# Attention stage of a macaron block: score and value units regrouped, projections in two banks and three units ahead, one denominator pass per sequence

## The reference

```python
x = x + 0.5 * ffn(_layernorm(x))
x = x + attn(_layernorm(x))
x = x + 0.5 * ffn(_layernorm(x))
...
# attn: 16 heads of 64
Q = _phi(h @ Wq); K = _phi(h @ Wk); V = h @ Wv     # _phi(x) = elu(x) + 1, h = layernorm of the layer's input
num = causal sum of (q . k) v;  den = max(causal sum of (q . k), EPS_DEN)
x = x + (num / den) @ Wo
x = x + gelu(_layernorm(x) @ Wf1) @ Wf2
```

## Time and profile before

| what | us |
|---|---|
| median of 3 runs | 2244.29 |
| lowest, highest | 2234.66, 2257.18 |
| the profiled execution | 2249.25 |
| its span, first to last instruction | 2246.5 |
| mean granted TensorE clock, share of full speed | 0.926 |

### The profile page before, as it was taken

The page is one execution under the profiler, slowest core; times in us unless marked ns, Lnnn a source line. Parts: engine busy times, 40 slices in busy tenths (PEclk is TensorE's granted clock), DMA queues, the critical chain, the costliest instruction groups (busy, mean ns, idle before and its releaser), DMA issues. The chain is left out here.

```text
span 2246.5 us, 36234 instructions
## 1 busy us (share of the span) xinstructions
PE 1800.2 (80%) x12619; PEld 1410.7 (63%) x12619; DVE 1527.2 (68%) x4255; ACT 1027.5 (46%) x1754; POOL 949.2 (42%) x1035
## 2 busy tenths in 40 slices
PE   3341799993999999999999999999984342999970
PEld 2231677772777777777777777777763232777750
DVE  6663577774777777777777777777756563777753
ACT  1210566662455554554555545545531111766650
POOL 5775255556232323322323323232215774455560
PEclk9999999996999999999999999999995555999995
DMA  5533566651000000000000000000000114566637
GB/s 159 174 123 110 198 241 238 228 196 52 11 6 11 10 6 11 11 6 11 11 6 11 6 10 11 1 1 1 1 1 29 45 49 166 197 225 226 227 133 228
DMA packets 89310, 190.29 MB, mean 85 GB/s; under 512 B 15869, under 2 KB 54442, under 8 KB 78122
## 3 DMA queue, kind: packets, MB, share of 16 engines
q1 hardware_dynamic: 60202, 141.68, 18.8%
q0 software_dynamic: 18176, 37.79, 4.9%
q10 hardware_dynamic: 10752, 8.52, 1.1%
HBM read 131.08 MB, written 56.85 MB: 84 GB/s over the span
## 5 line engine op out<-in xcount | busy, mean ns | idle before, releaser
L503 POOL DMA_INDIRECT expert_rows<-f_rows_out,f_dest x312 | 311.3, 998 | 304.3 <-DVE f_rows_out L722 231.4
L1273 DVE TENSOR_TENSOR at_sc<-at_s_ps,at_mask 128x384 f32<-128x384 f32 x516 | 262.9, 551 | 139.4 <-PE at_s_ps L944 134.3
L1087 ACT ACTIVATE at_exps<-at_proj_ps 128x512 f32<-128x512 f32 x258 | 153.5, 595 | 369.0 <-PE at_proj_ps L925 362.3
L1165 POOL TENSOR_TENSOR at_sc<-at_sc 128x512 f32<-128x512 f32 x129 | 177.1, 1373 | 306.4 <-DVE at_sc L1273 303.9
L497 POOL DMA_INDIRECT sent_rows<-f_xn,f_slot x256 | 251.1, 981 | 107.7 <-issue 73.0
L435 ACT ACTIVATE f_hid<-f_up_ps,f_w 128x512 f32<-128x512 f32 x312 | 214.6, 688 | 171.5 <-PE f_up_ps L344 149.2
L1267 DVE SCALAR_TENSOR_TENSOR at_qk<-at_exps,at_relus 128x512 f32<-128x512 f32 x260 | 208.6, 802 | 53.2 <-ACT at_relus L1088 53.0
L699 DVE TENSOR_TENSOR f_hid_lo<-f_hid,f_hid_hi 128x512 fp32r<-128x512 f32 x312 | 208.2, 689 | 14.5
L941 PE MATMUL at_s_ps<-at_qk 64*128 64x256 f32 x1032 | 181.3, 428 | 3.4 <-DVE at_sc L1273 2.7
L955 PE MATMUL at_num_ps<-at_sc,at_vals 128*64 128x256 f32 x1024 | 160.5, 392 | 0.0
L695 DVE CAST f_hid_hi<-f_hid 128x512 fp32r<-128x512 f32 x156 | 66.6, 427 | 132.9 <-issue 121.6
(11 more groups left out here) (263 smaller groups left out, 4523.9 us busy)
## 6 DMA issues: line engine op xcount, KB each, us to landing
f_w<-split_weights SPq DMA_DIRECT2D x78, 1028.0 KB
f_got<-sent_rows SPq DMA_DIRECT2D x78, 264.0 KB
split_weights<-f_split SPq DMA_DIRECT2D x8, 1024.0 KB
at_taken<-expert_rows SPq DMA_DIRECT2D x64, 128.0 KB, 2.1
f_w<-expert_rows SPq DMA_DIRECT2D x32, 256.0 KB, 4.1
expert_rows<-f_rows_out,f_dest POOLq DMA_INDIRECT x312
sent_rows<-f_pads ACTq DMA_DIRECT2D x16, 264.0 KB
x<-in_L_attn_x SPq DMA_DIRECT2D x16, 256.0 KB, 5.6
```

The source lines that it names most:

```text
L503: g.indirect_dma_start(out=k.back[:, :], out_offset=bass.IndirectOffsetOnAxis(dest[:, i % RING_DEST, q:q + 1], 0), in_=rows_out[:, i % RIN ...
L1087: A(exps[:, c % 2, :], bank[:, :], ACT.Exp).then_inc(s_exp, 1)
L1165: g.tensor_tensor(sc[:, par, :, 3, :], sc[:, par, :, 1, :], sc[:, par, :, 2, :], ALU.add).then_inc(s_sum, 1)
L1273: last = tt(flat(sc[:, par, 2 * cc + half, 0:3, :]), s_ps[2 * cc + half][:, 0:3 * P], flat(mask[:, :, :]), ALU.mult)
```

## The change

- PE's order in a unit becomes S, S, V, then qk, qk, v. S and V, which use the array in parts, stand together; the three projections, which use all of it, stand together. Most fills move into or behind the projections.
- The projections use two banks in turn (proj_ps[0], proj_ps[1]; the second is the former den_ps) and run three units ahead. A projection waits until the one before the last has been evacuated.
- denominators runs once for a sequence, with 16 matmuls, at u = 0 of the next one between the two S. It writes the bank num_ps, so it waits for the copy of the last V, and the next V waits for DVE to have read it (s_den). at_sc grows from 2 to 6 buffers for this; at_num moves into the spent raw1 and raw2.
- The iterations run to NB + 2 with what each has to do (has_z, has_rest, has_down), so nothing runs on zeros and nothing for sequences past the last; there is no separate tail. The fills' order is up2, b0, down, b1, b2, b3, out, z and an (one transposing fill), up0. The four final broadcasts, which had a bank each, go through at_slot_ps one by one.
- hT_hi and h2_hi are made by ACT with a second affine instead of a cast on DVE.
- POOL's memsets of gel, xa, num and y go. It clears the first FFN's semaphores after s = 0, not at the end.

```diff
-        proj_ps, num_ps, den_ps, slot_ps = ps("proj"), ps("num"), ps("den"), ps("slot")
+        proj_ps, num_ps, slot_ps = [ps(f"proj{i}") for i in range(2)], ps("num"), ps("slot")
...
+            def project(what):
+                n = number[what]
+                bank = proj_bank(n)
+                if n >= 6:
+                    pe.wait_ge(s_proj_out, n - 5 if n < 8 else n - 1)
...
+            def denominators(s):
+                pe.wait_ge(s_sum, UNITS * (s + 1))
+                pe.wait_ge(s_num_out, UNITS * (s + 1))
+                for u in range(UNITS):
+                    for j in range(4):
+                        last = mm(num_ps[32 * j:32 * j + 32, 0:BT], den_sel[:, u, :], sc[:, (UNITS * s + u) % RING_SC, j, 0:4:3, :],
+                                  start=(u == 0), stop=(u == UNITS - 1))
+                last.then_inc(s_quad, 1)
...
+                    if u == 2 and has_rest(s):
+                        pe.wait_ge(s_o, 4 * (s - 1) + 4)
+                        output_product((s - 1) % 2)
+                    if ("qk", g + 3, 0) in number:
+                        project(("qk", g + 3, 0))
+                    if u == 1 and has_rest(s):
...
+                        broadcast(1)
+                    if ("qk", g + 3, 1) in number:
+                        project(("qk", g + 3, 1))
+                    if u == 1 and has_rest(s):
+                        pe.wait_ge(s_o, 4 * (s - 1) + 2)
+                        broadcast(2)
...
+                    if u == 0 and has_rest(s):
...
+                        broadcast(0)
+                    if u == 1 and has_rest(s):
+                        pe.wait_ge(s_o, 4 * (s - 1) + 3)
                         broadcast(3)
...
+                    if ("qk", g + 3, 0) in number:
+                        phi(2 * (g + 3))
...
+                    if u == 1 and rest:
+                        weigh(s, 1)
...
+                    if u == 1 and rest:
+                        weigh(s, 2)
+                        weigh(s, 3)
```

More of the change, by code:

```diff
@@ L767 @@
 RING_TAKEN = 4
+RING_SC = 6
 def attention_phase(nc, k, spent):
@@ L848, in attention_phase, with projected, proj_bank, has_z @@
             sem("gelu"), sem("x"))
-        fills_before = (0, 2, 5, 7)
-        first_banks = [proj_ps, s_ps[0], s_ps[1], s_ps[2]]
-        first_fills = [("qk", 0), ("qk", 1), ("v", 0), ("qk", 2), ("qk", 3), ("v", 1)]
+        LAST = UNITS * NB
+        first = [("qk", 0, 0), ("qk", 0, 1), ("v", 0, 0, 0), ("qk", 1, 0), ("qk", 1, 1), ("qk", 2, 0), ("qk", 2, 1), ("v", 0, 0, 1)]
+        def projected(g):
+            s, u = g // UNITS, g % UNITS
+            there = [("qk", g + 3, cc) for cc in range(2) if g + 3 < LAST]
+            ahead = s + (u + 2) // UNITS
+            return there + ([("v", ahead, ((u + 2) // 2) % 2, u % 2)] if ahead < NB else [])
+        number = {what: n for n, what in enumerate(first + [w for g in range(LAST) for w in projected(g)])}
+        def proj_bank(n):
+            return (proj_ps + s_ps)[n] if n < 6 else proj_ps[n % 2]
+        def has_z(s):
+            return s + 2 < NB
+        def has_rest(s):
+            return 1 <= s <= NB
+        def has_down(s):
+            return 2 <= s <= NB + 1
+        def fills(s):
+            return (["up2"] * has_down(s) + ["b0"] * has_rest(s) + ["down"] * has_down(s) + ["b1", "b2", "b3", "out"] * has_rest(s)
+                    + ["z_an"] * (has_z(s) or has_rest(s)) + ["up0"] * has_rest(s))
+        def fill(s, what):
+            return 3 + sum(len(fills(i)) for i in range(s)) + fills(s).index(what)
         def xc(s, q=None):
@@ L913, in output_product @@
                         cols = slice((c % 2) * BT + q * P, (c % 2) * BT + (q + 1) * P)
[L914 removed]
+                        last = mm(slot_ps[:, q * P:(q + 1) * P], num[par][:, c // 2, cols], k.wo[:, c, :],
                                   start=(c == 0), stop=(c == PAIRS - 1))
                 last.then_inc(s_slot, 1)
[L918 to L925, removed]
[L926 removed]
@@ L968, in denominators @@
                 last.then_inc(s_quad, 1)
-            pe.sem_inc(s_quad, 1)
             pe.wait_ge(s_z, 1)
[L972 to L986, removed]
+            transpose_slot()
@@ new lines, in affine, with z_out, gelu @@
+            def affine(dst, g_col, bank, s):
+                A(dst, bank, ACT.Identity, bias=k.cols[:, g_col + 1:g_col + 2], scale=k.cols[:, g_col:g_col + 1]).then_inc(s, 1)
+            def z_out(i):
+                if i >= 1:
+                    act.wait_ge(s_hT_lo, i)
+                affine(hT[:, :], ROW_G1, slot_ps[:, 0:BT], s_hT)
+                affine(hT_hi[:, i % 2, :], ROW_G1, slot_ps[:, 0:BT], s_hT_hi)
+            def gelu(s, what, c):
+                act.wait_ge(s_slot, fill(s, what))
+                A(flat(gel[:, c:c + 2, :]), slot_ps[:, :], ACT.Gelu).then_inc(s_gelu, 1)
@@ new lines, in _ @@
+                    if u == 3 and ahead:
+                        hT_low(s + 2)
+                    if u == 2 and rest:
+                        dve.wait_ge(s_st["C"], s)
+                        aggregate("C")
+                    if ("qk", g + 3, 0) in number:
+                        phi(2 * (g + 3))
+                    if u == 0 and ahead:
+                        dve.wait_ge(s_st["A"], s + 3)
+                        aggregate("A")
+                    if u == 0 and rest:
+                        weigh(s, 0)
```

505 lines of the change are left out of this document (221 added, 284 removed).

## The result

| | before | after |
|---|---|---|
| median us (range, runs) | 2250.73 (2234.66 to 2265.46, 4) | 2300.07 (2290.30 to 2306.97, 4) |
| span of the profiled execution | 2246.5 | 2305.0 |
| from attention's first transposition to its last sum | 1142.3 | 1184.5 |

The ratio is 1.022, 95% interval 1.013 to 1.031: slower, though the interval leaves open whether by more than 2%, and the median is 2 us beyond the upper end of the predicted range. Run again, the same two kernels gave 1.017 (1.012 to 1.022).

A forecast was written before the change was run, and what follows sets the result against it. PE was taken to bound the loop. +29.0 for 29 sequences, -9.9, -1.8 and -4.0 for first, second and last, -1.2 start and +6.4 end gave +18.5: 2267.8 on the profiled execution, 2263 on the median; range 2215 to 2298.

The forecast's parts named there:

- Changes of shape and D: PE, whole-array to part-array switches: 24 a sequence become 12 at 0.2 each, plus 0.1 for lost exits: -2.5 us.
- the four restarts: PE: a matmul run that starts after a wait is 0.1 longer; four a sequence, +0.4 us, lower bound none.
- Rival 4: PE: the 0.2 belongs to blocks, not shape changes, so the 2.4 stay: +3.4 a sequence, 2333 us; chance 0.02.
- Rival 2: Part-array shapes follow each other freely and waits cost no restart: +0.3 a sequence, 2243 us, no change; chance 0.20.
- v, +1.45: PE's v waits for the first qk's bank: 0.64 at u = 2 and 0.8 at u = 0, a sequence.
- Rival 1: Two projection banks hide the evacuation, v never waits: a sequence at 33.7, 2215 us, faster; chance 0.17.
- b2 and b3, +2.0: At u = 1 b2 waits 1.75 for weigh(1), queued behind phi on DVE; b3 waits 0.25 for weigh(2).
- Rival 3: POOL's work falls on DVE's chain through their shared port: +0.7 before b2, 2295 us, clearly slower; chance 0.18.
- A sequence, +1.0: The loop's period: the terms sum to +1.05, taken as +1.0, 35.35 us, for 29 sequences +29.0.
- The tail, +6.4: From the last V's end to the last sum: 32 us instead of 25.7, broadcasts going one by one; +3 to +9.
- Start, first and last sequence: Outside the steady loop: start -1.2 (-4 to +3), first sequence -9.9, second -1.8, last -4.0 us.

The follow-up runs named there:

- the run with two more: Changed kernel with u = 2's first qk between the two scores, output product behind V: 35.735 us a sequence, against 35.36 with the output product between the two qk.
- the filled wait: Changed kernel with the second qk's six matmuls at u = 1 issued three times, ahead of b2: steady intervals 35.41 to 35.47 us, attention 1172.7.
- the longer one: Changed kernel with DVE making the phi ahead of weigh(1) twice, so b2 waits longer: 37.28 to 37.55 us in every steady interval.
- the tail's banks: Changed kernel with the last pass's b1 to b3 in three scores banks, ahead of the down product: last V to last sum 28.9 us, 8.8 less.

## Why the prediction was wrong

The direction and the two waits were right; the size was not. Attention became 42.2 longer, by the steps it should have been 18.5. Point by point:

- **Changes of shape and D, -2.5.** Held in the main: 0.19 a change by the run with two more, so 2.3 for the 12, and D's successor starts after 1.86 (1013.63 to 1015.49), the number predicted. The count of 24 before missed two: at u = 3 half of the up product stands between V and D. Added up by the starts of all blocks of one sequence (before from 1009.06, after from 1049.83), what is no wait became 1.8 less, or 2.2 without the four restarts: 0.3 under the 2.5. Rival 4 falls by this. Rival 2 falls by the period, 1.1 over before's instead of 0.3; V takes 1.45 behind scores as it did behind a projection, so S to V is not free.
- **v, +1.45.** Held: 0.63 + 0.76 = 1.39 against 0.64 + 0.8. Rival 1, that two banks hide the evacuation, falls. The Trainium skill, Perfetto Trace Analysis, Optimizing Tensor Performance, asks that independent matmul groups rotate through different banks, so that the evacuation of one overlaps the next group. The changed kernel does so, and the trace agrees in part: the waits L969 <- L1114 of 0.47 and 0.60 show that two banks in this order hid only part of the evacuation. The prediction called the rule the opposite of its reading, which is more than it says. Putting v first removed both waits without a third bank.
- **b2 and b3, +2.0.** Held: 1.55 for b2 (1.75 said), and 0.25 for b3 (1030.66 to 1031.61 less 0.70), as said. Rival 3's port was not in this chain: phi and weigh there took 0.69 and 0.68. That 2300 lies near its 2295 is chance. Of its two witnesses the cast in rows 10 is the weaker: it ended at 547.89, 1.84 behind the memset named, while POOL's other memsets ran on to 547.74.
- **A sequence, +1.0.** 35.45 instead of 35.35, 29 x 0.1 = 3 us. That it is so near is in part luck: the waits came out 0.3 smaller and the gain 0.3 smaller than said. PE was busy for 93%, not below 92%.
- **The step that failed: the sum has no term for the clock.** I priced b2's wait at its length. PE's granted clock falls behind it in seven sequences, 7 x 1.6 = 11.3 us. Shown by the filled wait (work added, none slow) and the longer one (every one slow). The profile of before could have warned. In its tail, behind an idle of 3.01 (though not behind the one of 2.05 before it), PE ran at the lower level:

```profile
1667.55 3.81 PE L914 MATMUL at_slot_ps<-wo,at_num 128*128 128x128 f32 x32 [2.05 <-DVE at_num L1280]
1674.37 0.69 PE L882 MATMUL at_slot_ps<-ident,at_an 128*128 128x128 f32 x2 [3.01 <-DVE at_an L1248]
```

```profile
1675.00:1680.00 5.00, 2.99 (x13) 2.64 (x12) 0.72 (x2) 1.69 (x3) 0.00 (x0) 0.50 0.00 0
```

- **The tail, +6.4.** +12.0 (37.7 for 25.7). The order and the waits were as said; what I left out is in the main again the clock, and 4 of the 8.8 us that the tail's banks gave back are that. The bound of +9 was too near.
- **Start, first and last sequence.** PE's first projection came 3.8 sooner (544.63 for 548.43), as said, but the first scores of the loop start at 560.65 for 560.91, 0.3 sooner instead of 1.2: PE waits 5.6 there, for what was not found out, and starts again at half clock (its first part takes 1.22, 0.77 before). The first sequence took 26.3, not 24.4, but before's own had been 35.9 and not the 34.35 that I set against it, so it gave 9.6 of the 9.9; the second gave 1.65 of 1.8. The last, to its last V, took 30.2 instead of 28.8, and before's 31.3 instead of 32.8: -1.1 for -4.0. Together +4.2.

The terms are 3 + 11.3 + 5.6 + 4.2 = 24.1, where 42.2 - 18.5 = 23.7 are to be explained. Of these the clock is 11.3 in the loop and some 4 in the tail; without the loop's share alone the median would lie within the range. What the medians differ by beyond that (49.3 against 42.2) is within the scatter outside attention.

## What to carry to other kernels

A wait that is new on the bound engine costs its length and perhaps, as here behind idles of 1.4 and 2.0 us before b2, the clock as well: look behind every idle of PE for longer durations of the same block, and price a reordering with and without. A queue's order on the engine that feeds PE (here one weigh behind one phi) can decide whether a reordering of PE pays (here 44 us of the 64 that 2.2 a sequence are worth); ask of each wait taken away which chain was just long enough before, since PE comes sooner to all of them.

## What was not expected of the hardware

- Before b2, an idle of TensorE of 1.39 brought the granted clock from 1.00 to 0.50 for some 3.4 us after some of its occurrences (3 to 7 of some 29, by the run), one of 2.00 after all, one of 0.89 after none. Length alone does not decide it: in the tail no fall came behind an idle of 2.05 (before) and one of 2.28 (the tail's banks). Why 1.39 does it in one sequence and not in the next stays open; the same sequences were slow when the changed kernel ran again, but only in part the same in the run of the tail's banks, whose loop is the same.
- Filling such an idle with matmuls whose result is thrown away made attention 11 us shorter.
- The code ahead of and behind attention, the same in all runs, took other times on other chips: attention began at 520 to 523 us on one and at 531 to 543 on the rest, and 554 to 584 us followed it.
